# GpSimd's gathers of embedding rows wait for z of the unit four ahead, in one place instead of two

## The chip, the core and the metric

The kernel runs on one core of a Trainium2 chip. The metric is the device time of one execution in microseconds. A core has five engines, each with its own instruction stream: TensorE (PE in the profile; its weight loads are PEld) multiplies matrices, VectorE (DVE) and ScalarE (ACT) do elementwise work and move results out of PSUM, GpSimd (POOL) here only issues the indirect loads of table rows, and SyncE (SP) issues all other transfers. The engines meet through semaphores: counters that one instruction raises and another waits for.

## The reference

A recommendation model's tower for 2048 samples, in fp32. For each sample 26 rows of 64 numbers are read from 26 tables by the sample's ids:

```python
e = stack([tbl_f[ids[:, f]] for f in range(26)], axis=1)        # 2048 x 26 x 64
x = layer_norm(dense @ Wd.T, gd, bd)                             # 2048 x 128
y = layer_norm(einsum('bnd,ed->bne', e, Ws), gs, bs)             # 2048 x 26 x 128
y = layer_norm(einsum('bne,pn->bep', y, Wsi), gsi, bsi)          # over p: 2048 x 128 x 32
T = concatenate([x[:, None, :], swapaxes(y, 1, 2)], axis=1)      # 2048 x 33 x 128
Z = einsum('bnd,bmd->bnm', T, T)                                 # all 33 x 33 products of a sample
out = layer_norm(Z[:, tril_i, tril_j] @ Wl.T, gl, bl) * mask     # 528 products -> 512, 384 used
h = relu(concatenate([out, dense], 1) @ W_top1 + b_top1)
h = relu(h @ W_top2 + b_top2);  result = h @ W_top3              # 2048 x 1
```

## The kernel before

The 2048 samples are 16 batches of 128, a batch is four **units** of 32 samples, so there are 64 units, k = 4n + j. A unit's table rows arrive by 8 gathers where j is 0 and by 6 where j is 1, 2 or 3 (26 a batch); each gather is one indirect load by GpSimd of 128 rows of 64 numbers into `rows[:, j, g, :]`. There are four such buffers, one for each j, so unit k writes over unit k-4.

TensorE's program is written out as **steps**, one for each unit, and step k works on three units at once. For unit k it transposes the gathered rows (`p_t`, line 520) and, once ScalarE has copied them (`et`, line 742), forms the quadratic form that gives the rows' variances (`p_q`, line 556, signal `q_done`). For unit k-1 it mixes the normalised rows with Wsi (`p_u`, lines 542 and 545, signal `u_done`); ScalarE rounds that to `ut_high` (line 755), VectorE makes the rest `ut_low` (line 1004), and TensorE multiplies both by Ws (`p_y`, lines 575 to 585, `y_done`). VectorE and ScalarE then normalise y and write `feat` (line 1050). For unit k-2 TensorE forms all products of each sample, **z**: 64 small matmuls one after the other (line 617, signal `z_done`), which ScalarE copies out (`zs`, line 809, the mark by which steps are counted below). One sample's z is

```python
last = nc.tensor.matmul(p_z[32 * s:32 * s + 32, SLOTS * g:SLOTS * g + SLOTS],
                        f[:, 2:SLOTS], f, start=True, stop=True)
```

TensorE's order within a step is fixed: p_t of unit k, p_u of unit k-1, p_q of unit k, p_y of unit k-1, z of unit k-2, and at the step's end a piece of the batch-wide layers of earlier batches. That piece depends on j: 20 matmuls of the first top layer at j = 0 and j = 1 (line 467), 16 of the second at j = 2 (line 654), 15 wide ones of the interaction layer at j = 3 (lines 484 to 489). At j = 3 the products of a batch, read back from memory by SyncE, are also copied by ScalarE (`zc`, lines 761 and 763) and transposed by TensorE (lines 597 and 602) ahead of z. Batches 2 to 14 run in a loop on every engine, one batch (four steps) a turn; the batches around it are written out.

GpSimd runs through all 64 units without a loop. Before each unit's first gather it waits for `rows_ready` (VectorE has normalised the rows of unit k-4, so the buffer is free) and for `z_done` to reach k-4, that is z of unit k-5, which is formed at the end of step k-3. Before the fifth gather (`g == 4`) it waits for `q_done` to reach k-1, that is p_q of unit k-2, in the middle of step k-2. From the fifth on it also waits until the gather four earlier in the same unit has landed. So in the steady state a step holds one group of four gathers behind the z that ended the step before, and a second group of two (four where j = 0) behind p_q.

Of the kernel before, what the change touches and what calls it, by code (L numbers as in the profile page):

```python
# [30 lines left out]
UB = 4  # L31
# [51 lines left out]
def landings(j, one, batches):  # L83

    return 16 * len(range(one, 2 * PAIRS[j], UNDER_WAY)) * batches
# [19 lines left out]
def dlrm_kernel(nc, a):  # L105

    scratch = nc.dram_tensor("products", (NB, 128, GB, SLOTS), F32, kind="Internal").ap()
    with ExitStack() as ctx:
# [6 lines left out]
        def sem(name):  # L115
            return ctx.enter_context(nc.semaphore(name))
# [139 lines left out]
        q_done = sem("q_done")  # L256
# [15 lines left out]
        z_done = sem("z_done")  # L272
# [39 lines left out]
        def after(eng, semaphore, count):  # L312

            if not isinstance(count, int) or count > 0:
                eng.wait_ge(semaphore, count)
# [119 lines left out]
        @block.gpsimd  # L435
        def _(pool):

            for n in range(NB):
                for j in range(UB):
                    k = UB * n + j  # L440
                    if k < 2:
                        pool.wait_ge(index_ready, k + 1)
                    elif k == UB:
                        pool.wait_ge(index_ready, 3)

                    after(pool, rows_ready, k - UB + 1)
                    after(pool, z_done, k - UB)
                    for g in range(2 * PAIRS[j]):
                        if g == 4:

                            after(pool, q_done, k - 1)
                        if g >= UNDER_WAY:

                            pool.wait_ge(gathered[j][g % UNDER_WAY], landings(j, g % UNDER_WAY, n) + 16 * (g // UNDER_WAY))
                        t = FIRST[j] + g // 2
                        pool.indirect_dma_start(  # L456
                            out=rows[:, j, g, :], out_offset=None, in_=a["table"],
                            in_offset=bass.IndirectOffsetOnAxis(ap=index[:, n, t, g % 2:g % 2 + 1], axis=0),
                        ).then_inc(gathered[j][g % UNDER_WAY], 16)
# [690 lines left out]
```

## Time and profile before

| | |
|---|---|
| runs of the kernel before | 766.05, 772.88, 775.83 us, median 772.88 |
| the profiled execution | 775.44 us |
| its span, first to last instruction | 773.6 us |
| mean granted TensorE clock | 0.861 of full |
| busy share of the span | PE 80%, PEld 65%, DVE 57%, ACT 35%, POOL 51% |
| chain of waits that ended last | PE 60%, issue 14%, another core or an unknown queue 12%, DVE 6%, ACT 4% |

The profiled execution is 2.6 us above the median of the runs and within their spread; 1.8 us of it lie outside the span. "Issue" in the chain is time in which an engine waited for nothing that the profile shows; "another core or an unknown queue" (in rows: "remote") is a wait whose release the profile cannot place at the end of an instruction. Busy times of TensorE count matmuls whose ends are modelled.

### The profile page before, as it was taken

Reading aid. Unit: us, or ns where it says so; the run is one execution under the profiler, and the core shown is the slowest. Engines: PE = TensorE matmul, PEld = TensorE weight load, DVE = VectorE, ACT = ScalarE, POOL = GpSimd, SP = SyncE. Lnnn points to the kernel's source line nnn. Section 1 sums busy time; section 2 is a strip of 40 time slices with the busy share of each in tenths; the row PEclk is TensorE's granted clock in tenths of the full one; section 3 lists DMA queues with packets and bytes.
Section 4 is the critical chain, followed back from the end, with each engine's and each line's share of the span. In section 5 each row is a group of like instructions: output and inputs, shape, how many; then the busy total and the mean of one; then the engine's idle time right before and its main releaser. Section 6 shows DMA issues by size and latency. Waiting matters only on the chain.

```text
span 773.6 us, 19159 instructions
## 1 busy us (share of the span) xinstructions
PE 618.4 (80%) x7293; PEld 506.1 (65%) x7293; DVE 443.2 (57%) x862; ACT 273.8 (35%) x647; POOL 397.1 (51%) x420
## 2 busy tenths in 40 slices
PE   2648678887988778797887889788788969788977
PEld 2535457776767667675666667677667757666766
DVE  5357847375655647565564656556464755647731
ACT  1014323333433343352333334333433534243622
POOL 6736654555555455546545455655555554555000
PEclk9759878798987989699998969889796978889989
DMA  3605423242232224233222323322232332224140
GB/s 76 192 15 104 58 43 48 41 57 47 40 54 42 46 42 55 49 46 48 41 46 42 55 46 41 56 44 48 38 55 47 48 50 46 41 39 55 34 44 2
DMA packets 97307, 39.04 MB, mean 50 GB/s; under 512 B 77314, under 2 KB 89218, under 8 KB 97282
## 3 DMA queue, kind: packets, MB, share of 16 engines
q1 hardware_dynamic: 83970, 25.07, 20.8%
q0 software_dynamic: 13312, 13.66, 9.9%
q8 instruction: 15, 0.25, 0.1%
q14 instruction: 10, 0.07, 0.1%
HBM read 29.76 MB, written 8.92 MB: 50 GB/s over the span
## 4 chain that ended last, share of the span: by engine, by line
PE 60%; issue 14%; another core or an unknown queue 12%; DVE 6%; ACT 4%; POOL 2%; DMA 1%; ACTq 0%; SPq 0%; DVEq 0%
PE p_z L617 9%; PE p_b L467 9%; PE p_u L545 6%; PE p_b L654 6%; PE p_y L581 4%; PE p_q L556 4%; PE p_t L520 3%; PE p_y L585 3%; PE p_b L484 2%; ACT ut_high L755 2%; PE p_y L575 2%; PE p_b L486 2%; DVE y_sum L1037 2%; POOL rows L456 2%
## 5 line engine op out<-in xcount | busy, mean ns | idle before, releaser
L456 POOL DMA_INDIRECT rows<-in_table,index x416 | 396.9, 954 | 318.6 <-PE p_z L617 101.3
L617 PE MATMUL p_z<-feat 128*32 128x34 f32 x4096 | 90.0, 216 | 66.1 <-issue 65.2
L617 PEld LDWEIGHTS p_z<-feat 128*32 128x32 f32 x4096 | 67.4, 124 | 97.4 <-issue 94.8
L1004 DVE TENSOR_TENSOR ut_low<-p_u,ut_high 128x512 fp32r<-128x512 f32 x64 | 44.2, 690 | 151.4 <-ACT ut_high L755 128.7
L545 PEld LDWEIGHTS p_u<-wsi_c,rows_n 128*128 128x128 f32 x512 | 88.1, 205 | 8.8 <-issue 5.6
L545 PE MATMUL p_u<-wsi_c,rows_n 128*128 128x192 f32 (+4 forms) x512 | 86.8, 314 | 4.0 <-issue 4.0
L1037 DVE TENSOR_REDUCE y_sum<-y_sq 128x32 f32<-128x1024 f32 x64 | 78.0, 1218 | 18.5 <-ACT y_sq L804 14.5
L742 ACT COPY et<-p_t 128x512 f32<-128x512 f32 (+1 forms) x64 | 32.4, 506 | 153.6 <-PE p_t L520 68.0
L1050 DVE TENSOR_TENSOR feat<-p_y,y_rs 128x1024 f32<-128x1024 f32 x64 | 78.4, 1225 | 9.1 <-DVE y_rs L1047 3.5
L755 ACT CAST ut_high<-p_u 128x512 fp32r<-128x512 f32 x64 | 37.5, 586 | 92.6 <-remote 58.1
L804 ACT ACTIVATE y_sq<-p_y 128x1024 f32<-128x1024 f32 x64 | 64.9, 1014 | 14.5 <-remote 11.1
L556 PE MATMUL p_q<-gram,et 128*128 128x128 f32 x416 | 61.9, 289 | 6.7 <-ACT et L742 5.4
L556 PEld LDWEIGHTS p_q<-gram,et 128*128 128x128 f32 x416 | 53.8, 199 | 9.9 <-ACT et L742 7.4
L467 PE MATMUL p_b<-hz,w 128*128 128x128 f32 x336 | 59.5, 322 | 0.0
L581 PE MATMUL p_y<-ut_high,wy_low 64*128 64x512 f32 x128 | 30.3, 470 | 36.5 <-ACT ut_high L755 35.6
L1047 DVE RECIPROCAL y_rs<-y_sd 128x32 f32<-128x32 f32 x64 | 22.3, 349 | 57.5 <-ACT y_sd L812 57.5
L467 PEld LDWEIGHTS p_b<-hz,w 128*128 128x128 f32 x336 | 51.2, 228 | 1.6
L654 PE MATMUL p_b<-h,w 128*128 128x128 f32 x224 | 51.0, 419 | 0.0
L520 PE MATMUL p_t<-eye,rows 128*128 128x128 f32 x208 | 40.0, 311 | 10.6 <-DMA rows<-in_table,index 7.7
L809 ACT COPY zs<-p_z 128x272 f32<-128x272 f32 x64 | 24.8, 388 | 65.4 <-PE p_z L617 65.1
L654 PEld LDWEIGHTS p_b<-h,w 128*128 128x128 f32 x224 | 47.1, 320 | 1.0
L796 ACT ACTIVATE sd_e<-var_g 128x8 f32<-128x8 f32 (+1 forms) x64 | 13.4, 210 | 88.0 <-issue 68.4
(140 smaller groups left out, 914.2 us busy)
## 6 DMA issues: line engine op xcount, KB each, us to landing
products<-zs SPq DMA_DIRECT2D x64, 136.0 KB
zb<-products SPq DMA_DIRECT2D x256, 34.0 KB
rows<-in_table,index POOLq DMA_INDIRECT x416
dense_x<-in_dense SPq DMA_DIRECT2D x16, 128.0 KB
wl<-in_Wl_rows SPq DMA_DIRECT2D x1, 1280.0 KB
w<-in_W SPq DMA_DIRECT2D x2, 512.0 KB
masks<-in_masks SPq DMA_DIRECT2D x1, 960.0 KB
w1z<-in_W SPq DMA_DIRECT2D x1, 768.0 KB
```

The source lines that it names most:

```text
L456: pool.indirect_dma_start(out=rows[:, j, g, :], out_offset=None, in_=a["table"], in_offset=bass.IndirectOffsetOnAxis(ap=index[:, n, t, g % ...
L467: last = nc.tensor.matmul(out, w1[:, c, 128 * m:128 * m + 128], hz[:, c, :] if c < 3 else dt_all[:, n - 2, c - 3, :], start=start and c == ...
L520: last = nc.tensor.transpose(p_t[:, 128 * m:128 * m + 128], rows[:, j, 2 * m:2 * m + 2, :].rearrange("r g d -> r (g d)"), eye[:])
L545: last = nc.tensor.matmul(p_u[:, NP * (lo - UH * of):NP * (hi + 1 - UH * of)], rows_n[:, t, :, :].rearrange("r h d -> r (h d)"), wsi_c[:, ...
L556: last = nc.tensor.matmul(p_q[:, 128 * m:128 * m + 128], et[:, m, :], gram[:], start=True, stop=True)
L581: nc.tensor.matmul(p_y[:, 512 * h:512 * h + 512], w[D * h:D * h + D, :], ut_high[D * h:D * h + D, :], start=False, stop=False)
L617: last = nc.tensor.matmul(p_z[32 * s:32 * s + 32, SLOTS * g:SLOTS * g + SLOTS], f[:, 2:SLOTS], f, start=True, stop=True)
L654: last = nc.tensor.matmul(p_b[:, 128 * m:128 * m + 128], w2[:, c, 128 * m:128 * m + 128], h1[:, c, :], start=c == 0, stop=c == 3)
L755: nc.scalar.copy(ut_high[:], p_u[:]).then_inc(ut_high_ready, 1)
L804: nc.scalar.activation(y_sq[:].rearrange("e b p -> e (b p)"), p_y[:], ACT.Square).then_inc(sq_ready, 1)
L1037: nc.vector.tensor_reduce(y_sum[:], y_sq[:], AX, ALU.add).then_inc(y_summed, 1)
L1050: nc.vector.tensor_tensor(feat[:, (j - 1) % UB, :, 2:SLOTS], p_y[:].rearrange("e (b p) -> e b p", p=NP), y_rs[:].unsqueeze(2).to_broadcast ...
```

## The change

The wait for `z_done` ahead of a unit's first gather goes. The wait for `q_done` ahead of its fifth becomes a wait for `z_done` to reach k-3, that is z of unit k-4, which is formed at the end of step k-2. The waits for `rows_ready` and for landings stay, and so do all gathers and their order.

```diff
                     after(pool, rows_ready, k - UB + 1)
-                    after(pool, z_done, k - UB)
                     for g in range(2 * PAIRS[j]):
                         if g == 4:
 
-                            after(pool, q_done, k - 1)
+                            after(pool, z_done, k - 3)
                         if g >= UNDER_WAY:
 
                             pool.wait_ge(gathered[j][g % UNDER_WAY], landings(j, g % UNDER_WAY, n) + 16 * (g // UNDER_WAY))
```

`after` waits only where the count is above zero, so units 0 to 3 are gathered without this wait.

## Rows read from the trace of the kernel before

**Rows 1.** page, part 5: line engine operation, count, busy and mean; idle before, releaser

```profile
L456 POOL DMA_INDIRECT rows<-in_table,index x416 | 396.9, 954 | 318.6 <-PE p_z L617 101.3
L617 PE MATMUL p_z<-feat 128*32 128x34 f32 x4096 | 90.0, 216 | 66.1 <-issue 65.2
```

**Rows 2.** view of line 456: duration ns min/median/max; idle before it, us and times

```profile
L456 POOL DMA_INDIRECT rows<-in_table,index x416: 941/947/2601, 3.5 to 715.0; - x139
...
  PE p_q L556: 66.9, 36
```

**Rows 3.** timeline, GpSimd, one step: start us, length us, operation, [idle before <-releaser]

```profile
403.64 0.94 POOL L456 DMA_INDIRECT rows<-in_table,index  x1 [1.96 <-PE p_z L617]
...
407.39 0.94 POOL L456 DMA_INDIRECT rows<-in_table,index  x1 [0.31 <-issue]
409.73 0.95 POOL L456 DMA_INDIRECT rows<-in_table,index  x1 [1.40 <-PE p_q L556]
...
413.49 0.95 POOL L456 DMA_INDIRECT rows<-in_table,index  x1 [0.31 <-issue]
```

**Rows 4.** timeline, ScalarE, the four steps of one loop turn

```profile
402.90 0.39 ACT L809 COPY zs<-p_z 128x272 f32<-128x272 f32 x1
...
406.45 0.48 ACT L742 COPY et<-p_t 128x384 f32<-128x384 f32 x1 [1.93 <-PE p_t L520]
409.42 0.59 ACT L755 CAST ut_high<-p_u 128x512 fp32r<-128x512 f32 x1 [2.49 <-remote]
...
416.02 0.39 ACT L809 COPY zs<-p_z 128x272 f32<-128x272 f32 x1 [2.88 <-PE p_z L617]
...
422.23 0.59 ACT L755 CAST ut_high<-p_u 128x512 fp32r<-128x512 f32 x1 [0.92 <-issue]
...
426.54 0.40 ACT L809 COPY zs<-p_z 128x272 f32<-128x272 f32 x1
...
432.95 0.59 ACT L742 COPY et<-p_t 128x512 f32<-128x512 f32 x1 [4.49 <-remote]
...
438.40 0.39 ACT L809 COPY zs<-p_z 128x272 f32<-128x272 f32 x1 [0.49 <-PE p_z L617]
...
444.88 0.59 ACT L755 CAST ut_high<-p_u 128x512 fp32r<-128x512 f32 x1 [3.22 <-remote]
...
448.60 0.39 ACT L809 COPY zs<-p_z 128x272 f32<-128x272 f32 x1
```

**Rows 5.** timeline, TensorE, p_u and z of the same step

```profile
406.42 1.23 PE L545 MATMUL p_u<-wsi_c,rows_n 128*128 128x128 f32 x8
...
411.21 0.79 PE L617 MATMUL p_z<-feat 128*32 128x34 f32 x41
412.50 0.24 PE L617 MATMUL p_z<-feat 128*32 128x34 f32 x2 [0.50 <-issue]
...
413.98 0.27 PE L617 MATMUL p_z<-feat 128*32 128x34 f32 x5 [0.55 <-issue]
415.43 0.48 PE L617 MATMUL p_z<-feat 128*32 128x34 f32 x15 [1.18 <-issue]
```

**Rows 6.** timeline, TensorE, z after the last gather

```profile
723.68 0.77 PE L617 MATMUL p_z<-feat 128*32 128x34 f32 x64
```

**Rows 7.** windows: length, busy of PE PEld DVE ACT POOL, granted clock, DMA share

```profile
411.00:414.50 3.50, 1.69 (x51) 1.00 (x49) 2.89 (x6) 1.34 (x3) 2.82 (x3) 1.00 0.16 28
414.50:421.50 7.00, 6.07 (x40) 6.02 (x41) 1.58 (x2) 1.62 (x5) 3.78 (x4) 0.51 0.16 40
```

**Rows 8.** timeline, ScalarE, an early step with six gathers in a row

```profile
100.79 0.39 ACT L809 COPY zs<-p_z 128x272 f32<-128x272 f32 x1 [6.04 <-PE p_z L617]
...
104.16 0.59 ACT L755 CAST ut_high<-p_u 128x512 fp32r<-128x512 f32 x1 [2.06 <-issue]
...
110.69 0.39 ACT L809 COPY zs<-p_z 128x272 f32<-128x272 f32 x1 [0.46 <-PE p_z L617]
```

**Rows 9.** timeline, GpSimd, the sixth of those gathers

```profile
107.78 0.94 POOL L456 DMA_INDIRECT rows<-in_table,index  x1 [0.30 <-issue]
```

## The prediction

> **What bounds the kernel now.** I read the list of costly groups first, then the view of the gathers' line, then the timelines of GpSimd, ScalarE and TensorE over one loop turn, side by side, and the windows with the granted clock last.
>
> GpSimd looks harmless in the list: 416 gathers, 396.9 us busy and 318.6 idle ahead of them [rows 1]. The line to stop at is z: TensorE stood idle 66.1 us ahead of z matmuls, 65.2 of them "issue", with no engine to blame [rows 1]. The timeline shows when. In the step at 411 us the first 41 matmuls of z go in 0.79 us, then 8 trickle out until 415.43, and the last 15 go at once [rows 5]. The same 64 take 0.77 us in one piece after the last gather [rows 6]. The trickle begins when a second group of four gathers (409.73 to 414.44) is under way and ends 1.0 us behind it [rows 3, 5]. So gathers under way starve z.
>
> They do a second thing. The eight parts of p_u run from 406.42 to 407.65 [rows 5], but ScalarE starts on their result at 409.42, released by "remote" [rows 4]: 1.09 us after the fourth gather of the first group ended at 408.33 [rows 3]. The loop turn shows this at each step: from zs to the next signal that matters it is 6.52, 6.21, 6.41 (here et, the signal of p_t) and 6.48 us [rows 4], though the layer pieces ahead of p_u differ. A group of four starts 0.74 us behind zs and lasts 4.70 (three pitches of 1.25 and 0.95), so it ends at 5.44, and the signals come about 1.1 later. TensorE's signals are **held** until the gathers pause. How they are held the trace does not say, only when they are let go.
>
> A turn from zs to zs is 13.12, 10.52, 11.86 and 10.20 us, together 45.70 [rows 4]. The path is: z, the first gather group, its release, p_y, z; it is set by when GpSimd's groups end as much as by TensorE. GpSimd's busy half hides that.
>
> **The change, part by part.** *The wait at the first gather goes.* Alone this would let the first four gathers of a unit start right behind the last of the unit before. Nothing has to be paid for it in buffers: rows_ready of unit k-4 is a step old by then.
>
> *The fifth gather waits for z instead of q.* The two stops a step become one, behind z. From the stop follow the last two or four gathers of a unit and the first four of the next without a pause: groups of 8, 6, 6 and 6 a turn in place of eight groups (4 and 2, and once 4 and 4). The 8 follow the z of a j = 0 unit, in the second step of the turn at 402.90. The gathers themselves cost what they did: 947 ns, 941 at the least [rows 2]. The stop at q that goes had GpSimd idle for 66.9 us in all [rows 2], worth nothing, since GpSimd is not late. The last gathers of a unit are now issued in the step before their use, within 5 us of its beginning, so landing is not late either. Queued behind the new wait are only gathers; the time it costs is in what TensorE can do meanwhile.
>
> What is **gained**: no gather runs from a step's release to its z, so z goes in 0.8 to 0.9 us. The stall of z is 3.7 us in the first step of the turn (411.21 to 415.91, less 1.0) [rows 5]; the 65.2 us in all [rows 1] over 14 turns are 4.7 a turn, so the other three steps have a third of a microsecond each.
>
> What is **paid**: a group of six ends at 0.74 + 7.20 = 7.94 behind zs, its release is at 9.04; a group of eight ends at 10.44, release 11.54. The release was at 6.5. So the held signals are 2.5 us late in three steps and 5.0 in one, 12.6 us a turn, if they are held to the end. From the signal to the next zs the rows give 6.60, 4.31, 5.45 and 3.72 [rows 4]; without the stalls 2.9, 4.0, 5.1 and 3.4.
>
> The trace of before has no steady step with a long group, so how much passes inside one is unknown. **Upper bound**, all held to the end: 9.04 + 2.9, 11.54 + 4.0, 9.04 + 5.1, 9.04 + 3.4 = 54.1 a turn, 8.4 more. **Lower bound**, nothing but z held: each step ends 0.4 us behind its release, 9.4, 11.9, 9.4 and 9.4 = 40.1, 5.6 less. **The value I take**: matmuls pass at the rate at which they trickled in z, 8 in 2.9 us or 2.7 per us [rows 5]. p_t is through at 3.55 us behind zs (et at 406.45 [rows 4]); the 9 matmuls of p_u then take 3.3 us, u_done at 6.9; the 6 of p_q take 2.2 more and are through at about the release, 9.04. Left behind it are p_y (from ut_high 409.42 to z at 411.21 was 1.8, of which 0.6 was ScalarE's, now done before: 1.2), z and the signal, 1.0: the first step is 11.2, the last likewise 11.3. In the second, 11.54 + 2.0 = 13.5 (zc and its transposes pass during the group). In the third more matmuls stand ahead of p_q and et is itself held, so p_q comes only at the release, and from it to zs I leave 3.6 of the 5.1: 12.6. Together 48.6, that is 2.9 more. It is nearest to the row of z, the only one that counts matmuls passing under gathers in the steady state.
>
> Unlike turns do not matter: the written-out steps from the fourth on behave like the loop's. There are 60 units after the fourth, 15 turns; the last unit's gathers end at 716, and the first turn has no layer pieces, so I count 14. 14 x 2.9 = **41 us**. At the start, the last four gathers of unit 4 move from behind q to behind the first z, at most 3 us once, and nothing at the end; I leave both out. The profiled execution of 775.4 becomes 816; it lies 2.6 above the median, so the run becomes 814.
>
> The clock: TensorE was granted 1.00 in the window in which z stalled and 0.51 in the 7 us behind it [rows 7], so idle time is paid again as half speed, and half the 6.07 us of work there is 3 us. Before, the stall of z did this once a turn, now the hold in the middle of each step may, with z at full speed. I set one against the other at nothing.
> The Trainium skill's page "TensorE: Matmul & The Clock Gate", section "HAM oscillation — how this bites in real kernels", says that a loop whose work is shorter than the wait between pieces starts every piece at the low clock. Rows 7 agree for one stall, and the rule speaks against this change: it makes one long wait a step of two short ones.
>
> **The rivals.**
> *Held to the end* (0.16): for it, three steps of four before are released within 0.15 us of 1.1 behind their group, not earlier; against it, z does trickle. 8.4 x 14 = 118 us, 891.
> *Cold behind each hold* (0.10): p_y and z, 2.0 us in a step at full clock, at half speed in all four steps, and the layer piece as well where it isn't hidden: 0.8 to 1 us a step, 3.2 to 4 a turn on top of the 2.9, about 90 us, 860. This is the rule of the page as a mechanism of this kernel.
> *A swap* (0.16): if matmuls pass at 3.5 per us instead of 2.7, the first, third and last steps lose 0.6 to 0.9 each and the second 1; the turn is 45.7 again and what z gains is what the holds cost. 773, within 757 and 788.
> *Free but for z* (0.24), the other side: an early step with six gathers in a row, from 101.53 to 108.72, got ut_high at 104.16, only 3.4 us behind zs, and lasted 9.90 [rows 8, 9]. If steady steps behave so, z alone waits for the group and the turn is 40.1 to 43: 2.7 to 5.6 less, 38 to 78 us less, 695 to 735; where it holds in part, up to 757. It decides from the point where p_u is signalled before about 5 us behind zs. Against it: that step belongs to a batch without a top-layer piece, so p_u came 2 us earlier than in the steady steps, in all of which it was late.
> That the stop doesn't bind can be left out: GpSimd reaches the fifth gather with its step's z still 2 us or more off.
>
> **How the numbers follow.** The likeliest case (0.34) is some holding, 790 to 840 us. About 2% is what a measurement of this kernel can tell from no change: 757 and 788. Slower by more: 0.34 + 0.16 + 0.10 = 0.60. Within: 0.16. Faster: 0.24. The range takes in the likeliest case, the swap, the cold clock and the weaker half of the free case: 732 to 872. Left out are the free case at its best (about 0.10) and most of holding to the end (0.10).
>
> **What would show it.** GpSimd's idle time released by p_q is zero, that by z is up, and its timeline has groups of six and eight. z takes 0.8 to 1.1 us in every step, and idle "issue" ahead of it falls from 65 us to under 15. ut_high stands at 7 to 9 us behind zs in place of 6.5. The steps of a turn are about 11.2, 13.5, 12.6 and 11.3. I am wrong if ut_high comes at 5 or earlier (free), or if z still stalls at the end of the groups: then TensorE got there first, and GpSimd is the bound.

## The result, and the profile after

The changed kernel takes 823.34 us (median of 5 runs, 818.01 to 827.92) where the kernel before took 772.88: a ratio of 1.065, interval 1.060 to 1.071. It is **slower**, as forecast, and 9 us above the forecast of 814. The profiled execution took 826.89 us, its span is 825.0 us and its mean granted clock 0.863.

From the page of the changed kernel, first the chain of waits, then three of the costliest groups (columns as in [rows 1]; lines 455, 616 and 555 are 456, 617 and 556 of before):

```profile
PE 49%; another core or an unknown queue 18%; issue 13%; DVE 10%; ACT 7%; POOL 2%; DMA 1%; ACTq 0%; SPq 0%; DVEq 0%
...
L455 POOL DMA_INDIRECT rows<-in_table,index x416 | 400.5, 963 | 369.1 <-PE p_z L616 257.9
...
L616 PE MATMUL p_z<-feat 128*32 128x34 f32 x4096 | 71.2, 224 | 28.4 <-issue 28.2
...
L555 PE MATMUL p_q<-gram,et 128*128 128x128 f32 x416 | 64.6, 297 | 20.5 <-issue 14.1
```

TensorE's idle "issue" ahead of z fell from 65.2 us [rows 1] to 28.2, in the direction forecast. It did not come under 15, and some came back ahead of p_q: 14.1 us. The chain has 18% "another core or an unknown queue" where before had 12%: the signals that the profile can't place.

What released GpSimd at line 455, us and times, the line on z:

```profile
  PE p_z L616: 257.9, 60
```

The 66.9 us of idle time by p_q [rows 2] are gone; all 60 stops are at z.

The timeline of GpSimd over one turn of the changed kernel, the first gather and the last of each group:

```profile
195.63 0.94 POOL L455 DMA_INDIRECT rows<-in_table,index  x1 [4.93 <-PE p_z L616]
...
204.37 0.94 POOL L455 DMA_INDIRECT rows<-in_table,index  x1 [0.30 <-issue]
...
215.50 0.94 POOL L455 DMA_INDIRECT rows<-in_table,index  x1 [0.30 <-issue]
...
228.26 0.94 POOL L455 DMA_INDIRECT rows<-in_table,index  x1 [0.30 <-issue]
...
237.48 0.94 POOL L455 DMA_INDIRECT rows<-in_table,index  x1 [0.30 <-issue]
```

That is a group of 8 and three of 6 (over the whole trace 15 and 44, by my count of gathers less than 0.45 us apart). The end of a group is the start of its last plus 0.94: 205.31, 216.44, 229.20 and 238.42.

ScalarE over the same turn, to be held against those ends (it answers to [rows 4]; y_row is the signal of a top layer's last matmuls):

```profile
195.72 0.38 ACT L808 COPY zs<-p_z 128x272 f32<-128x272 f32 x1
...
201.33 0.59 ACT L754 CAST ut_high<-p_u 128x512 fp32r<-128x512 f32 x1 [1.89 <-remote]
...
207.12 0.26 ACT L727 COPY y_row<-p_b 1x128 f32 x1 [3.82 <-remote]
...
209.03 0.39 ACT L808 COPY zs<-p_z 128x272 f32<-128x272 f32 x1 [0.17 <-PE p_z L616]
...
216.46 0.59 ACT L741 COPY et<-p_t 128x512 f32<-128x512 f32 x1 [5.55 <-remote]
...
218.10 0.59 ACT L754 CAST ut_high<-p_u 128x512 fp32r<-128x512 f32 x1 [0.87 <-remote]
...
221.99 0.38 ACT L808 COPY zs<-p_z 128x272 f32<-128x272 f32 x1
...
225.42 0.59 ACT L754 CAST ut_high<-p_u 128x512 fp32r<-128x512 f32 x1 [0.85 <-PE p_u L544]
...
231.37 0.38 ACT L808 COPY zs<-p_z 128x272 f32<-128x272 f32 x1
...
239.88 0.59 ACT L754 CAST ut_high<-p_u 128x512 fp32r<-128x512 f32 x1 [3.87 <-remote]
...
243.49 0.38 ACT L808 COPY zs<-p_z 128x272 f32<-128x272 f32 x1
```

The steps are 13.31, 12.96, 9.38 and 12.12 us, together 47.77. ut_high is 5.6, 9.1, 3.4 and 8.5 us behind its zs. In the turn of [rows 4] the steps of the same order had 6.2, 7.1, 6.5 and 6.5. And TensorE, z and p_u of the same turn:

```profile
207.83 1.14 PE L616 MATMUL p_z<-feat 128*32 128x34 f32 x64
...
214.14 1.31 PE L544 MATMUL p_u<-wsi_c,rows_n 128*128 128x64 f32 x8
...
220.54 0.77 PE L616 MATMUL p_z<-feat 128*32 128x34 f32 x64
...
227.83 0.57 PE L616 MATMUL p_z<-feat 128*32 128x34 f32 x22
...
230.38 0.59 PE L616 MATMUL p_z<-feat 128*32 128x34 f32 x38 [1.17 <-issue]
...
235.43 1.23 PE L544 MATMUL p_u<-wsi_c,rows_n 128*128 128x128 f32 x8
...
241.96 1.13 PE L616 MATMUL p_z<-feat 128*32 128x34 f32 x64
```

Three things are seen here. In the second step p_u is through at 215.45, but ScalarE gets word at 218.10, 1.66 us behind the end of the group; in the fourth at 236.66, and word at 239.88, 1.46 behind. In the first step the eight gathers let ut_high pass in the middle, but the y_row signal came only at 207.12, 1.81 behind the group's end, and the last p_b and z waited for it. In the third step p_u got through: ut_high came at 3.4 us, TensorE reached z inside the group, and z stalled, 22 matmuls in 0.57 us and the last ones at 230.38, 1.18 us behind the group's end. So all four steps are still let go by the end of a group of gathers, three through a signal and one through z.

The release is not always behind the end, and it is not only ScalarE that waits. In the second step et started at 216.46, at the very end of its group. In the third the last matmul of p_q was through at 226.11, and VectorE started on it at 228.94:

```profile
228.94 0.56 DVE L1008 TENSOR_TENSOR prod<-p_q,rows 128x384 f32<-128x384 f32 x1 [1.60 <-remote]
```

The trace also holds the times at which semaphores were raised, which no row here prints. Taken over the twelve turns between the zs of units 8 and 56: 191 signals of TensorE's are recorded whose last matmul was through inside a group of gathers, and 154 of them were raised more than 0.3 us later, at a median of 2.59 us over the 191 and 6.58 us at most. Of the 399 signals of ScalarE and VectorE inside groups none was later than 0.01 us. So it is TensorE's signals that are late, whoever waits for them. Two things limit this reading. The ends of matmuls are modelled, so a late signal can't be told from a matmul that was itself finished late. And records are missing: 41 more signals of TensorE's inside groups have none, outside groups none is missing. The recording of the trace thus suffers in the same stretches, and whether it has a part in the holding is open, since no run is on record that is known to have gone without it.

The granted clock of two windows of this turn (the third number from the end), the hold ahead of ut_high, and z with what follows it:

```profile
237.69:241.96 4.27, 1.65 (x8) 0.59 (x6) 1.43 (x3) 1.80 (x6) 0.73 (x1) 0.92 0.25 54
241.96:245.80 3.84, 3.84 (x84) 3.77 (x83) 2.86 (x7) 1.72 (x4) 1.89 (x2) 0.65 0.15 45
```

After the hold the work runs at 0.65. Taken over z alone the granted clock is 0.50 in the first and fourth steps, where z takes 1.14 and 1.13 us, and 1.00 in the second, where it takes 0.77. Over the whole execution the clock is what it was, 0.863 for 0.861.

The balance of the trade stands in ScalarE's waits: engine, what it waited in, releaser, us in total, times, longest. The kernel before:

```profile
ACT zs L809 <- PE p_z L617: 65.1, 28, 6.0
...
ACT ut_high L755 <- remote: 58.1, 19, 3.3
...
ACT et L742 <- remote: 24.9, 6, 4.5
```

and the changed kernel:

```profile
ACT ut_high L754 <- remote: 83.5, 28, 5.1
...
ACT et L741 <- remote: 56.3, 11, 6.6
...
ACT y_row L727 <- remote: 48.2, 13, 4.6
...
ACT zs L808 <- PE p_z L616: 8.7, 11, 3.5
```

ScalarE waited 56.4 us less for z, and y_row's 48.2 us are new (before, no such wait). The waits of ut_high and et that are labelled "remote" grew by 56.8 us, but part of that is only a new label: with every releaser taken together, the idle time ahead of ut_high went from 92.6 to 112.2 us and that ahead of et from 153.6 to 146.6. These waits overlap with other work and don't add up to the 51.5 us between the two executions, but they name the two sides.

**Per turn.** Between the zs of units 8 and 56 lie twelve turns: 539.7 us before and 584.8 after, so 44.98 and 48.73 a turn, 3.75 more. Fourteen times that is about 52 us, the whole difference. Means of the steps of these twelve turns, sorted by the unit whose zs begins them:

| step begins at zs of a unit with j = | before | after | forecast | ut_high behind zs, before and after | z at the step's end, before and after |
|---|---|---|---|---|---|
| 3 | 13.2 | 12.1 | 11.2 | 6.5, 8.3 | 4.66, 1.12 |
| 0 (group of 8) | 10.3 | 13.2 | 13.5 | 5.9, 5.3 | 1.38, 1.37 |
| 1 | 11.0 | 13.1 | 12.6 | 6.7, 8.9 | 1.33, 0.77 |
| 2 | 10.5 | 10.4 | 11.3 | 6.0, 5.2 | 2.41, 2.51 |

The last step has two forms: 9.4 us in 8 of 12 turns, with ut_high at 3.4 and a z that stalls and takes 3.1 to 3.4 us, and 12.4 in the others, with ut_high at 8.8.

### The profile page after: what moved, and what is told of

It reads as the page before. It is cut to its first block, busy times and chain, and to the rows that moved or that the text cites. A ratio compares the mean times of both kernels' runs of the same rounds, so it can differ in the third digit from the quotient of the medians.

```text
span 825.0 us, 19098 instructions
## 1 busy us (share of the span) xinstructions
PE 624.3 (76%) x7293; PEld 505.0 (61%) x7293; DVE 445.9 (54%) x862; ACT 270.6 (33%) x647; POOL 400.7 (49%) x420
## 3 DMA queue, kind: packets, MB, share of 16 engines
q0 software_dynamic: 13312, 13.66, 7.9%
## 4 chain that ended last, share of the span: by engine, by line
PE 49%; another core or an unknown queue 18%; issue 13%; DVE 10%; ACT 7%; POOL 2%; DMA 1%; ACTq 0%; SPq 0%; DVEq 0%
PE p_b L466 8%; PE p_z L616 6%; PE p_u L544 5%; PE p_b L653 4%; PE p_b L483 4%; PE p_y L580 3%; PE p_q L555 3%; PE p_b L485 3%; PE p_t L519 2%; PE p_y L584 2%; DVE y_sum L1036 2%; PE p_b L488 2%; ACT y_sq L803 2%; POOL rows L455 2%
## 5 line engine op out<-in xcount | busy, mean ns | idle before, releaser
L616 PE MATMUL p_z<-feat 128*32 128x34 f32 x4096 | 71.2, 224 | 28.4 <-issue 28.2
L616 PEld LDWEIGHTS p_z<-feat 128*32 128x32 f32 x4096 | 58.0, 133 | 50.8 <-issue 48.5
L741 ACT COPY et<-p_t 128x512 f32<-128x512 f32 (+1 forms) x64 | 32.3, 504 | 146.6 <-remote 56.3
L555 PE MATMUL p_q<-gram,et 128*128 128x128 f32 x416 | 64.6, 297 | 20.5 <-issue 14.1
L754 ACT CAST ut_high<-p_u 128x512 fp32r<-128x512 f32 x64 | 37.5, 586 | 112.2 <-remote 83.5
L1008 DVE TENSOR_TENSOR prod<-p_q,rows 128x512 f32<-128x512 f32 (+1 forms) x64 | 37.5, 585 | 48.1 <-remote 38.6
L466 PE MATMUL p_b<-hz,w 128*128 128x128 f32 x336 | 62.6, 335 | 0.0
L466 PEld LDWEIGHTS p_b<-hz,w 128*128 128x128 f32 x336 | 54.3, 240 | 1.4
L580 PEld LDWEIGHTS p_y<-ut_high,wy_low 64*128 64x128 f32 x128 | 13.3, 205 | 63.7 <-ACT ut_high L754 54.2
L519 PE MATMUL p_t<-eye,rows 128*128 128x128 f32 x208 | 35.7, 285 | 14.4 <-DMA rows<-in_table,index 7.6
L584 PE MATMUL p_y<-ut_low,wy_high 64*128 64x512 f32 x128 | 34.3, 532 | 11.0 <-DVE ut_low L1003 5.8
L811 ACT ACTIVATE y_sd<-y_sum,eps_col 128x32 f32<-128x32 f32 x64 | 20.6, 322 | 64.2 <-DVE y_sum L1036 64.2
```

The costliest lines, as they stand in the source:

```text
L466: last = nc.tensor.matmul(out, w1[:, c, 128 * m:128 * m + 128], hz[:, c, :] if c < 3 else dt_all[:, n - 2, c - 3, :], start=start and c == ...
L519: last = nc.tensor.transpose(p_t[:, 128 * m:128 * m + 128], rows[:, j, 2 * m:2 * m + 2, :].rearrange("r g d -> r (g d)"), eye[:])
L555: last = nc.tensor.matmul(p_q[:, 128 * m:128 * m + 128], et[:, m, :], gram[:], start=True, stop=True)
L580: nc.tensor.matmul(p_y[:, 512 * h:512 * h + 512], w[D * h:D * h + D, :], ut_high[D * h:D * h + D, :], start=False, stop=False)
L584: last = nc.tensor.matmul(p_y[:, 512 * h:512 * h + 512], wy_high[D * h:D * h + D, :], ut_low[D * h:D * h + D, :], start=False, stop=True)
```

## The experiments

The theory: gathers by index under way on GpSimd hold TensorE's signals and starve its small matmuls until the group is over, so longer groups cost more in signals than they give back in z. The rivals: the time lies in the waits' places as such; it is TensorE's clock; it is the traffic of the transfers, whoever starts them; or GpSimd's transfers of any kind do it. The experiments ran on five chips, named A to E in the order of the runs, and this turned out to matter (whether the chip of the result, called the first chip below, is one of them is not on record). The kernel before took 763.85 us on A (762.19 to 769.64), 591.11 on B, 589.23 on C, 774.56 on D (771.47 to 775.29) and 589.37 on E. Each ratio is against the kernel before on the same chip. The only traces of the kernel before and of the changed kernel where signals are held come from the first chip; where their steps are set beside those of a run on A, this may be a comparison of two chips.

### Without the gathers (chip A)

The kernel before, with GpSimd's loop cut to the first batch, and TensorE waiting for gathers in that batch alone:

```diff
-            for n in range(NB):
+            for n in range(1):
...
-                        for one in range(UNDER_WAY):
+                        for one in range(UNDER_WAY) if n == 0 else ():
```

> The kernel before, with the table rows gathered for the first batch alone; all later batches compute on those rows, and neither GpSimd nor TensorE waits for the gathers left out. Holding theory (gathers under way starve z and hold back TensorE's signals until the group ends): ut_high comes 4 to 5 us behind zs in place of 6.5, every z takes 0.8 to 1.1 us, a turn of four steps falls from 45.0 to about 31 us (the steps behind the last gather took 7 to 8 us before), and the run to 560 to 620 us. Late rows (the rows arrive late for the transposes, and that is all that the gathers cost): TensorE waited 7.7 us for them in all, so 755 to 773 us.

Measured: 574.62 us, ratio 0.750 (0.744 to 0.756), as the holding theory had it. Its chain of waits and its z:

```profile
PE 55%; DVE 26%; ACT 8%; issue 5%; POOL 2%; DMA 1%; another core or an unknown queue 1%; DVEq 0%; ACTq 0%; SPq 0%
...
L617 PE MATMUL p_z<-feat 128*32 128x34 f32 x4096 | 49.9, 200 | 0.0
```

Nothing stalls in z, "another core or an unknown queue" is 1%, and a turn is 31.05 us with steps of 7.0, 9.8, 7.6 and 6.7. TensorE bounds it. So of the 45 us of a turn before, about 14 are what gathers under way cost, and the clock goes with them: 0.967 for 0.861. Those 14 us have in them what TensorE lost at the lower clock; no run separates that share. This does not yet say whether it is the gathers or their traffic.

### Five gathers, then the stop at q (chip A)

```diff
-                        if g == 4:
+                        if g == 5:
```

on the kernel before: one gather more in the first group, one less in the second.

> The kernel before, with the stop at q ahead of the sixth gather and not the fifth: groups of five and one (five and three where j is 0). Holding theory: the first group ends 1.25 us later, so the signals come at 7.8 us behind zs in each step, 5.0 a turn; z wins back 1.25 us in the step with eight gathers and 0.3 in the others, 2.2 a turn; 2.8 a turn, 39 us, about 812 (795 to 815 if some signals pass early). Late rows: one gather in six moves, and to an earlier place: 773.

Measured: 783.68 us, ratio 1.024 (1.017 to 1.030): slower, as the holding theory had it, but by half of what it priced (20 us for 39, and below its 795 to 815). z and ut_high on its page:

```profile
L617 PE MATMUL p_z<-feat 128*32 128x34 f32 x4096 | 79.5, 218 | 38.0 <-issue 37.3
...
L755 ACT CAST ut_high<-p_u 128x512 fp32r<-128x512 f32 x64 | 37.5, 586 | 125.6 <-remote 92.5
```

This is the trade in small. z's idle time fell from 66.1 to 38.0 us, and the kernel is 2.4% slower: ut_high stands 7.3 and 7.2 us behind zs in the steps that begin at j = 1 and j = 3, where it stood at 6.7 and 6.5 (means of the traces), a part of the 1.25 us by which the first group is longer. In the other two it hardly moved (5.5 for 5.9 at j = 0, 6.5 for 6.0 at j = 2), and the expectation had the full 1.25 us in all four. The turn is 45.5 us against 45.0 on the first chip, which would make 7 us in all; the rest of the 20 is not accounted for, since A has no trace of the kernel before. Who looks only at the stall of z would call this a gain.

### One stop, at q (chip A)

The changed kernel, with the fifth gather waiting for q as before, and no wait for z. Against the kernel before, this is the first half of the change by itself:

```diff
-                            after(pool, z_done, k - 3)
+                            after(pool, q_done, k - 1)
```

> The kernel before without the wait for z: one stop a step, at q, with groups of six and eight behind it. Every gather is issued earlier than in the changed kernel. Holding theory: z falls into the group each step and creeps until 1.1 us behind its end; a step is 0.4 + 7.2 + 1.1 from q to z's end and 4.8 from there to the next q, 13.5, and 16 with eight gathers: 52 to 57 a turn, 870 to 940 us, slower than the changed kernel. Late rows: rows come earlier than in the changed kernel, so between 773 and 823. Clock alone (the time is lost only because TensorE's clock falls): like the changed kernel, since it also has one long pause a step, 810 to 835.

Measured: 1058.61 us, ratio 1.382 (1.374 to 1.390), far beyond what was expected. GpSimd and z on its page:

```profile
L455 POOL DMA_INDIRECT rows<-in_table,index x416 | 404.1, 971 | 593.5 <-PE p_q L555 480.9
L616 PE MATMUL p_z<-feat 128*32 128x34 f32 x4096 | 152.8, 207 | 234.8 <-issue 234.7
```

and TensorE's z in one of its steps, in which a group of six gathers ran from 510.55 to 517.84:

```profile
512.56 0.51 PE L616 MATMUL p_z<-feat 128*32 128x34 f32 x35
513.27 0.27 PE L616 MATMUL p_z<-feat 128*32 128x34 f32 x3 [0.20 <-issue]
...
516.19 0.25 PE L616 MATMUL p_z<-feat 128*32 128x34 f32 x3 [0.52 <-issue]
517.62 0.29 PE L616 MATMUL p_z<-feat 128*32 128x34 f32 x5 [1.18 <-issue]
519.05 0.42 PE L616 MATMUL p_z<-feat 128*32 128x34 f32 x10 [1.15 <-issue]
```

The groups are as long as in the changed kernel (45 of 6 and 15 of 8), they only begin in the middle of the step. ut_high comes free of them, 3.7 us behind zs in this step, and z runs right into them: 35 matmuls in half a microsecond and 29 more in 6.4 us, the last piece 1.21 us behind the group's end. A turn was expected at 52 to 57 us and is 64.8; z is 5.9 to 6.9 us long (means of the four steps), and the granted clock fell to 0.785. The expectation had the mechanism and not the size. Late rows (773 to 823) and the clock alone (810 to 835) are out as the whole cause. What it shows is that **where** in the step a group lies weighs more than how many stops there are: groups of the same lengths behind z cost 6.5% on the first chip, behind q 38% on A.

### The first wait kept beside the new one (chip A)

The changed kernel with the old first wait put back; against the kernel before, this is the second half of the change by itself. Since the unit before has already waited for a later z, this wait is always over when GpSimd comes to it:

```diff
+                    after(pool, z_done, k - UB)
```

> The changed kernel with the wait for z ahead of the first gather kept. Both theories: that wait asks for z of unit k-5, which the fifth gather of the unit before has already waited for, so nothing changes: 823 us, ratio 1.06 to 1.07. If removing it had a part in the loss, this one would be nearer to 773.

Measured: 791.35 us, ratio 1.033 (1.027 to 1.039). By both theories it should have been the changed kernel's 1.065. z:

```profile
L617 PE MATMUL p_z<-feat 128*32 128x34 f32 x4096 | 77.6, 219 | 56.4 <-issue 56.2
```

The groups are the same, 44 of 6 and 15 of 8, and the turn is 45.8 us for 48.7: the step with the group of 8 has ut_high at 4.6 and a z of 3.1 us (means), and the last step is in its short form every time. So the same order of gathers stands in more than one pattern, of which one passes p_u before it is held; and the two traces differ by 3 us a turn. Whether the chip or the added instruction picks the pattern is **open**: no run of the changed kernel is on record from A, and the two kernels met on no chip that holds signals. For the same reason the 6.5% itself is shown on the first chip alone; this near relative of the changed kernel lost 3.3% on A.

### The changed kernel again (chips B and C)

> The changed kernel itself once more, beside the next one. Keeping the wait for z ahead of the first gather gave 1.033 where the changed kernel gave 1.065, though that wait is always fulfilled and the groups were of six and eight in both. If the difference lies between chips or allocations: 1.03 to 1.04 here. If it lies in the code: 1.06 to 1.07 again.

> The changed kernel once more. On the chip of the last call the kernel before took 591 us and the change did nothing (1.0009), on the first chips 764 and 773 us. Where the kernel before takes over 750 us, signals are held, and the changed kernel is at 1.06 to 1.07; where it takes about 590, nothing is held, GpSimd's own 26 gathers a turn are the bound (32.5 us), stops do nothing, and it is at 1.00. A ratio of 1.03 on a chip with holding would mean that the jumps differ from chip to chip, and that keeping the wait for z did nothing.

Measured on B: 594.03 us, ratio 1.001 (0.995 to 1.007). On C: 589.74 us, ratio 0.999 (0.996 to 1.003), the second case of the later expectation. The same programs, both of them, ran in three quarters of the time. The page of C:

```profile
POOL 44%; issue 20%; DMA 17%; PE 13%; DVE 5%; ACT 2%; SPq 0%; POOLq 0%; DVEq 0%; ACTq 0%
...
L455 POOL DMA_INDIRECT rows<-in_table,index x416 | 399.0, 959 | 138.9 <-issue 116.5
...
L616 PE MATMUL p_z<-feat 128*32 128x34 f32 x4096 | 56.6, 201 | 0.2
```

and GpSimd's timeline there, two gathers out of a row without a pause:

```profile
309.57 0.94 POOL L455 DMA_INDIRECT rows<-in_table,index  x1 [0.30 <-issue]
310.82 0.94 POOL L455 DMA_INDIRECT rows<-in_table,index  x1 [0.30 <-issue]
```

A gather takes what it took, 0.94 us every 1.25. But z hardly stalls beside them (0.2 us in all), no signal of TensorE's in the twelve turns is more than 0.58 us late, the granted clock is 0.973, and now GpSimd is the bound: 26 gathers of 1.25 us are 32.5 us a turn, and the turn is 32.8. GpSimd stands at the stop at z once in the whole execution there, 1.7 us, so the change can't do anything. The slowdown belongs to chips that hold.

### The wait for rows_ready written twice (chip B)

```diff
                     after(pool, rows_ready, k - UB + 1)
+                    after(pool, rows_ready, k - UB + 1)
```

> The changed kernel with its wait for rows_ready ahead of each unit written twice, so that GpSimd has as many waits as with the wait for z kept. If one more waiting instruction between two gathers is what helped (it moves GpSimd against TensorE by some tens of ns, and the hold lets go in jumps): like that kernel, 1.03 to 1.04. If not, like the changed kernel in the same call.

Measured: 594.61 us, ratio 1.006 (1.002 to 1.011). It was meant to tell whether an instruction that waits for nothing picks the pattern of the kernel with the first wait kept. On a chip that holds nothing the question has no answer. The same holds for the next.

### The first wait kept, once more (chip E)

> The changed kernel with the always fulfilled wait for z ahead of the first gather kept, once more: 1.033 on its first chip. On a chip that holds signals (before over 750 us): 1.03 again if the difference to 1.065 is one of code (how GpSimd falls against TensorE), 1.06 to 1.07 if it is one of chips. On a chip without holding (before about 590): 1.00.

Measured: 590.94 us, ratio 1.002 (0.998 to 1.006). Nothing is held on E either.

### The rows by SyncE's plain transfers (chip B)

On the kernel before, the rows of all but the first batch loaded by SyncE from consecutive rows of the table, behind rows_ready (so it does not compute the reference):

```diff
+                        for g in range(2 * PAIRS[to]):
...
+                            sp.dma_start(rows[:, to, g, :], a["table"][128 * (8 * to + g):128 * (8 * to + g) + 128, :]
+                                         ).then_inc(loaded[to][g % UNDER_WAY], 16)
```

> The kernel before, with the rows of all batches but the first brought by SyncE, with as many transfers of the same size (128 rows of 256 bytes, plain and not by index, so that later batches compute on other rows), issued at the end of a step for the unit three ahead; GpSimd issues none after the first batch. If it is the transfers' traffic that starves z and holds signals: a turn of 43 to 47 us, 745 to 800 us in all. If it is the software side (GpSimd making the descriptors and their rings): a turn near the 31.0 of the kernel without gathers, 575 to 640 us.

Measured: 607.4 us, ratio 1.028 (1.013 to 1.043). z is clean, but so it is on B with gathers. What costs here is something else: the chain has DMA 40% and SyncE's queue 21%, and the first step of a turn (j = 0) is 9.3 us for 7.0 without gathers. ScalarE waited 30.8 us in 15 waits for the products read back, which now share SyncE's queue with the rows. It tells nothing on the theory.

### The rows by GpSimd's plain transfers (chips B, C and D)

The changed kernel, each gather by index replaced by a plain transfer of the same size into the same buffer, from consecutive rows (so it does not compute the reference):

```diff
-                        pool.indirect_dma_start(
-                            out=rows[:, j, g, :], out_offset=None, in_=a["table"],
-                            in_offset=bass.IndirectOffsetOnAxis(ap=index[:, n, t, g % 2:g % 2 + 1], axis=0),
+                        pool.dma_start(
+                            out=rows[:, j, g, :],
+                            in_=a["table"][128 * (8 * k + g):128 * (8 * k + g) + 128, :],
```

> The changed kernel with each gather replaced by a plain transfer of 128 table rows, still issued by GpSimd in the same places (so the rows are others). If the software side holds TensorE whatever the transfer: groups of six still hold the signals to their end, and the time follows the length of one issue, 780 to 830 us if it is about 0.95 us as before. If it is the lookup by index that costs: 575 to 650 us.

> The changed kernel with plain transfers of table rows issued by GpSimd in place of gathers, once more. On the chip without holding it took 558 us. If the chip holds signals under gathers of GpSimd's and any transfer that GpSimd makes does it: over 650 us there. If it is the work of the lookup by index that holds: 555 to 580 us on any chip.

> The changed kernel with plain transfers of table rows issued by GpSimd in place of gathers; on two chips without holding it took 558 us. Where the kernel before takes over 750 us: over 650 us if any transfer that GpSimd makes holds TensorE's signals, 555 to 600 us if only the gathers by index do. Where the kernel before takes about 590: 558 again, and the question stays open.

Measured: 558.34 us on B (ratio 0.945, 0.932 to 0.958), 557.57 on C (0.944, 0.935 to 0.953) and 557.71 on D (0.721, 0.716 to 0.726). D is the one that decides, because there the kernel before takes 774.56 us. GpSimd and z on its page:

```profile
L455 POOL DMA_DIRECT2D rows<-in_table x416 | 219.5, 535 | 281.0 <-PE p_z L616 255.2
...
L616 PE MATMUL p_z<-feat 128*32 128x34 f32 x4096 | 49.8, 200 | 0.0
```

and GpSimd's timeline, a group of eight:

```profile
320.23 4.21 POOL L455 DMA_DIRECT2D rows<-in_table  x8 [3.53 <-PE p_z L616]
```

The stops are the changed kernel's, at z, in groups of 6 and 8. The queue moved the same 13312 packets and 13.66 MB. z takes 0.77 us in each step, ut_high has no "remote" wait, and the turn is 31.05 us, that of the kernel without gathers. Of TensorE's 89 signals inside these groups in the twelve turns none is late. So neither this number of bytes and packets nor a transfer of GpSimd's as such holds TensorE: **the gathers by index do**. What it is in them stays open, since two more things changed. A group of eight is 4.2 us long here and 9.7 with indices, so a plain transfer occupies GpSimd for 0.53 us in place of 1.25. And the plain transfers read consecutive rows, the gathers scattered ones; plain transfers of scattered rows have no run.

No run that computes the reference is faster than the kernel before on its chip. A split of five only where j = 0 has no run.

## Why the prediction was right, and where it was not

**What bounds the kernel.** Right in kind. The signals let go by the groups' ends and the starved z were read off the trace, and the run without gathers puts their cost at about 14 of 45 us a turn. Plain transfers of the same size don't do it, which the trace of before could not tell.

**The first wait goes; the stop at q, worth nothing.** In the changed kernel GpSimd stands where it was forecast: all 60 waits are at z, and landings held back TensorE for 7.6 us in two places only. But neither wait was worth nothing. With the first gone and the stop at q kept the kernel took 38% more on A, because the groups then run into z. With the first kept beside the new one it lost 3.3% there, and whether dropping it costs the rest of the 6.5% is open.

**Gained: z.** Half right. It was to take 0.8 to 1.1 us in every step and its "issue" to fall under 15 us. In three steps of four it runs in 0.77 to 1.14 us, in all but two of the 36 steps of the twelve turns, and "issue" is 28.2 us. The step that begins behind z of j = 2 failed: the forecast had its p_u wait in the group, and in 8 of 12 turns p_u got through before it was held, as in the early step of [rows 8]. Then z stalls in the group instead. This is the rival "free but for z", in one step of four, and the step is 9.4 us as that rival had it. The forecast named the sign by which to know it (ut_high before 5 us), and took one behaviour for all steps.

**Paid: the held signals.** Right in two of three steps of six. ut_high at 8.3 and 8.9 us behind zs for the forecast 7 to 9; the release came 1.4 to 1.7 us behind the group for the 1.1 of before. That the sum of the two came out near 9.04 is luck: the forecast let a group start 0.74 us behind zs, and in the changed kernel it started between 0.4 us before and 0.2 us behind it, so groups of six ended at 6.8 to 7.4 and not at 7.94. In the step with the group of eight, p_u was signalled in the middle of the group (in the turn shown 1.6 us late), and y_row's signal was held in its place, to the same effect: 13.2 for 13.5.

**The value between the bounds.** 48.6 us a turn was forecast and 48.73 measured, between 40.1 and 54.1. The four steps are off by +0.9, -0.3, +0.5 and -0.9 and nearly cancel, so the agreement is better than the reasoning. The term that made the value was wrong in kind: matmuls were to trickle through a group at 2.7 a microsecond, and the nine of p_u to take 3.3 us. In the turn shown the eight of p_u go inside groups in 1.31 and 1.23 us, as fast as before; only their signal is late. Only z trickles, and at no fixed rate: with the stop at q 19 of its matmuls passed between 513.27 and 519.05, or 3.3 a microsecond. In the first step of the forecast the release came 0.7 us early (8.3 for 9.04) and from there to zs it took 3.8 us for the 2.2 left to it.

**The sum.** 2.9 us a turn became 3.75, 41 us became 52. Most of this is the base: the one turn of [rows 4] is 45.70 us, and the mean of twelve is 44.98. Of the 0.85 missing, 0.72 are that: the base was mis-sized, and taking the turn from twelve would have shown it.

**The clock.** Set at nothing, and the mean did not move (0.861, 0.863). After a hold it does fall: z takes 1.13 us at a granted 0.50 in the fourth step shown, as TensorE's work did before behind the stall [rows 7]. The second step's z, behind a hold too, ran at 1.00. The Trainium skill's page "TensorE: Matmul & The Clock Gate", section "HAM oscillation — how this bites in real kernels", says that short pieces behind longer waits each start at the low clock. The trace agrees for the first and fourth steps and not for the second, and the rival *cold behind each hold*, 860 us, is out.

**Held to the end** (891) is out: ut_high passes inside a group in two of the four steps of the turn shown. **A swap** (773) is out on the first chip, though the kernel with the first wait kept, at 45.8 us a turn and 3.3% on A, is nearer to it.

**What the prediction had no place for** is that on B, C and E hardly anything is held. There the answer is "no change", for a reason that isn't in the trace of before.

## What to carry to other kernels

If another engine's results arrive late and "remote", lay its queue of indirect transfers beside them and measure from the end of each group: a distance that repeats points to the cause, and a run without the transfers, or with plain ones, shows it. Then keep such groups short, and out of the phases of many small matmuls; a stall that goes in one place is worth nothing until it is known what the same group delays in its new one. Take the base of a sum from many turns, and measure a change of a few per cent on more than one chip before it is called a rule.

## What the runs showed of the hardware

- While GpSimd issues gathers by index, TensorE's signals to ScalarE and VectorE come late, up to 6.6 us in the changed kernel, while those of ScalarE and VectorE come within 0.01 us. ut_high came mostly 1.1 to 1.3 us behind the end of a group of four and 1.4 to 1.7 us behind one of six; some signals pass inside a group. The last packets of a group end about 1.1 us behind GpSimd's last instruction in both kernels, so a hold that lasts until the data are moved would fit the groups of four and falls short behind the longer ones; no run decides it.
- The same gathers starve small matmuls: 29 of z in 6.4 us, where 64 take 0.77. With plain transfers by GpSimd, of the same size and from consecutive rows, neither happens: 557.71 us for 774.56 on the same chip.
- It depends on the chip. The kernel before takes 764 to 775 us on the first chip, A and D and 589 to 591 on B, C and E, with the same gathers of 0.94 us every 1.25. Why the chips differ is open: no run here tells it.
- The same groups of gathers settle in patterns that differ by 3 us a turn (48.7 on the first chip, 45.8 on A with one wait more). What picks the pattern is open.
- A plain transfer of 128 pieces of 256 bytes takes GpSimd 0.53 us, a gather of the same 1.25.
